# One block for layers 2 and 3 of a four-layer image kernel: offsets, sampling weights and padded images of layer 3 made during layer 2's attention

## The chip, the cores and the metric

The kernel runs on one core of one Trainium2 chip. Its time is the device time of one execution in microseconds (us); lower is better. Times are medians of repeated runs on the chip, and the profile is one execution taken by the hardware profiler. The engines are TensorE (PE, whose weight loads the trace lists as PEld), VectorE (DVE), ScalarE (ACT), GpSimd (POOL) and SyncE (SP, which issues DMA transfers here). Each engine runs its own instruction list in order and meets the others at semaphores.

## The reference

The input is 16 images of 64 channels and 16 x 16 places, in float32. Four layers follow each other, each as `x = x + layer(norm(x))`, where the norm is a group norm over pairs of channels of one image:

```python
x = x + _L0_conv_ref(_gn(x), ...)        # pointwise conv, mixture of basis functions
x = x + _L1_conv_ref(_gn(x), ..., 16, 16) # depthwise conv and linear state mixing
x = x + _L2_conv_ref(_gn(x), ...)        # attention, 8 heads of 8, over the 256 places of an image
x = x + _L3_conv_ref(_gn(x), ...)        # deformable 3 x 3 convolution
```

Layer 2 is `softmax(q k^T / sqrt(8)) v` for every image and head, and a projection. Layer 3 makes, by an ordinary 3 x 3 convolution of the normed image, two offsets and one mask (a sigmoid) for each of nine taps and each place. It then samples the normed image at the shifted, fractional places (bilinear), multiplies by the mask, and contracts the nine taps and 64 channels with a weight. Everything is per image: no image's result needs another image.

## The kernel before

Two images lie in one tile of 128 partitions (64 channels each), so there are 8 pairs of images. The layers run one after the other, each in a block with one instruction list per engine.

**Layer 2 (`layer2`, lines 761 to 1105).** The queries and keys are split into bfloat16 parts, stored to DRAM and loaded back as stacks (`k_st`, `q_st`). Then one pipeline runs over steps `v` from -19 to 143, eight steps per image, the same loop on every engine. At step `v` TensorE makes the scores that give the row maxima of step `v + 19` (line 1034) and the scores of step `v` (line 1047), and in four of eight steps the product of exponents and values (line 1067). VectorE takes the maxima (line 910), ScalarE the exponents (line 965). Each image's maxima go by POOL (lines 869, 871) and four small DMAs on SP (line 837) back into a row of `q_st`; SP then waits until they have landed, and step 8 of the image's scores may not start before. Maxima end at step 108, scores at step 127. Line 929 adds the attention of one image to `x`.

**Layer 3 (`layer3`).** It begins when layer 2's block has ended. A group norm of all images is followed by padded copies (`xpad`), which DMAs lay out as `stack`, four images a group. `conv_offsets(g)` (lines 1463, 1465) makes a group's offsets and masks. A chunk is four images too. For a chunk, hats are computed: `relu(1 - |position - row or column|)` for each tap and place (ACT lines 1376 and 1382), times the mask, then split into three bfloat16 parts (ACT, with POOL or DVE) and sent by DMA as `hats`. Positions reach `hat` by DMA through DRAM (`load_positions`, `load_masks`); only two thirds of the first chunk's are spread by matmuls instead (lines 1472, 1477).

The sampling loop runs over 8 pairs `n` and 9 taps `t`: TensorE spreads the hats (lines 1500, 1510), ACT copies one product (line 1404), DVE multiplies (line 1335), and TensorE contracts (line 1523). In six taps of each pair it also weighs the next pair's image (line 1491). A chunk serves two pairs; its hats are made by ACT and POOL while the chunk before is sampled.

## Time and profile before

| | us |
|---|---|
| median of 3 runs | 527.64 (525.78 to 527.82) |
| the profiled execution's span | 528.0 |
| attention pipeline, from its first exponent to the last addition | 233.7 to 347.2 |
| from there to the first multiplication of the sampling loop | 347.2 to 383.6 |
| sampling loop, to its last addition | 383.6 to 522.8 |
| the result to DRAM | 522.8 to 528.0 |

| engine | busy us | share of span |
|---|---|---|
| PE | 439.1 | 83% |
| DVE | 342.4 | 65% |
| ACT | 288.9 | 55% |
| POOL | 132.8 | 25% |

Shares over the whole span say little here, since the stages differ. The rows further down are read by stage. A timeline row gives the start, the duration, the engine and line, the operation, and in square brackets how long the engine sat idle before it and what ended that. A matmul of float32 appears as two records.

### The profile page before, as it was taken

The numbers are of one execution on the slowest core, as the hardware profiler recorded it, in microseconds if no ns is written. First come the engines' busy times: TensorE is split into PE (matmuls) and PEld (weight loads), VectorE is DVE, ScalarE is ACT, GpSimd is POOL, SyncE is SP. The second block draws the span as 40 slices with busy tenths as digits, with TensorE's granted clock in tenths as the row PEclk, the third lists the DMA queues.
The fourth block names the chain that finished last, engine by engine and source line by source line (L and its number), as shares of the span: only waits on it lengthen the run. The fifth ranks groups of instructions, "written<-read, shape, count | busy, mean of one in ns | idle before, by whom it ended". The sixth has DMA issues, their size and how long they took to land. (4 is left out here: it accounts for less than half of the span.)

```text
span 528.0 us, 9368 instructions
## 1 busy us (share of the span) xinstructions
PE 439.1 (83%) x3406; PEld 231.3 (44%) x3406; DVE 342.4 (65%) x668; ACT 288.9 (55%) x511; POOL 132.8 (25%) x162
## 2 busy tenths in 40 slices
PE   0527768899999887679999999939898999999995
PEld 0216648555455664223333333324443454454442
DVE  4549876233344568978999996251654778777784
ACT  1279955131532437047878778722865578486441
POOL 4420004000000005744422212031364428065000
PEclk9956997999999988559999999957977999999999
DMA  5500000900000004952200000016390480933302
GB/s 142 164 0 1 0 0 1 197 1 1 0 1 0 1 0 107 279 175 67 73 27 3 3 2 4 0 47 160 100 226 15 89 181 2 217 55 68 67 2 79
DMA packets 20767, 33.79 MB, mean 64 GB/s; under 512 B 5657, under 2 KB 15497, under 8 KB 19957
## 3 DMA queue, kind: packets, MB, share of 16 engines
q1 hardware_dynamic: 16724, 23.70, 18.9%
q0 software_dynamic: 2176, 6.35, 4.3%
q10 hardware_dynamic: 1824, 3.19, 2.3%
q8 instruction: 26, 0.43, 0.4%
q14 instruction: 17, 0.13, 0.1%
HBM read 16.21 MB, written 4.64 MB: 39 GB/s over the span
## 5 line engine op out<-in xcount | busy, mean ns | idle before, releaser
L1335 DVE TENSOR_TENSOR L_s<-L_row_ps,L_cols 128x1024 f32<-128x1024 f32 x72 | 87.6, 1218 | 9.3 <-PE L_row_ps L1500 7.5
L910 DVE TENSOR_REDUCE L_mx<-L_ring 128x2 f32<-128x512 f32 x128 | 83.3, 686 | 12.4 <-PE L_ring L1034 11.8
L965 ACT ACTIVATE L_e<-L_ring 128x512 f32<-128x512 f32 x128 | 73.7, 597 | 21.4 <-PE L_ring L1047 19.3
L1523 PE MATMUL L_acc<-L_s,L_t_sb 128*64 128x256 f32 x576 | 81.6, 406 | 1.1 <-DVE L_s L1335 1.0
L1404 ACT ACTIVATE L_cols<-L_col_ps 128x512 f32<-128x512 f32 x72 | 42.8, 596 | 48.9 <-PE L_col_ps L1510 48.5
L1034 PE MATMUL L_ring<-stacks_k_st,stacks_q_st 64*128 64x256 bf16 x256 | 51.0, 301 | 7.0 <-DMA stacks_k_st<-L_k_parts 4.7
L1523 PEld LDWEIGHTS L_acc<-L_s,L_t_sb 128*64 128x64 f32 x576 | 36.0, 140 | 35.9 <-DVE L_s L1335 19.8
L1047 PE MATMUL L_ring<-stacks_q_st,stacks_k_st 64*128 64x256 bf16 x256 | 47.2, 282 | 1.2 <-DMA stacks_q_st<-L_m_parts 1.2
L1500 PE MATMUL L_row_ps<-L_hats,L_sel 48*128 48x512 bf16 x144 | 44.6, 392 | 0.0
L1067 PE MATMUL L_ctx_ps<-L_e,L_v_x 128*32 128x256 f32 x512 | 41.5, 398 | 0.0
L1311 DVE COPY L_t_sb<-L_acc 128x192 f32<-128x192 f32 x48 | 17.1, 357 | 31.4 <-PE L_acc L1491 31.4
L1034 PEld LDWEIGHTS L_ring<-stacks_k_st,stacks_q_st 64*128 64x128 bf16 x256 | 15.9, 98 | 43.8 <-DVE L_mx L910 24.2
L382 PE MATMUL L_y<-L_t,all_w_post 128*128 128x256 f32 x96 | 25.3, 418 | 11.5 <-DVE L_t L342 11.5
L1510 PE MATMUL L_col_ps<-L_hats,L_sel 48*128 48x512 bf16 x72 | 28.7, 400 | 7.0 <-DMA L_hats<-L_parts 5.0
L1491 PE MATMUL L_acc<-all_w_all,L_xn 64*128 64x192 f32 x96 | 26.8, 362 | 5.0 <-DVE L_t_sb L1311 2.7
L382 PEld LDWEIGHTS L_y<-L_t,all_w_post 128*128 128x128 f32 x96 | 19.4, 208 | 17.1 <-DVE L_t L342 14.2
L1491 PE MATMUL L_col_ps<-all_w_all,L_xn 64*128 64x192 f32 x96 | 26.7, 360 | 0.0
L853 POOL MEMSET L_v_x<- 128x1024 f32 x1 | 1.0, 951 | 101.7 <-POOLq L496 101.7
L1200 POOL TENSOR_TENSOR L_hat<-L_hat,L_mask 64x768 f32<-64x768 f32 x9 | 16.3, 1812 | 40.1 <-ACT L_hat L1382 40.1
L415 ACT ACTIVATE L_uu<-L_z,L_minus_mu,L_inv 128x256 f32 x48 | 24.4, 586 | 1.3 <-DVEq L314 1.3
L633 ACT ACTIVATE L_sq<-L_t_ps 128x1024 f32<-128x1024 f32 x4 | 4.1, 1024 | 34.9 <-PE L_t_ps L716 34.9
L656 PE MATMUL L_xs_ps<-L_stack,L_w_tap 128*128 128x512 f32 x48 | 22.7, 601 | 0.0
(270 smaller groups left out, 814.2 us busy)
## 6 DMA issues: line engine op xcount, KB each, us to landing
L_hats<-L_parts SPq DMA_DIRECT2D x28, 216.0 KB, 5.0
L_hat<-L_offsets SPq DMA_DIRECT2D x20, 192.0 KB, 4.7
L_mask<-L_offsets SPq DMA_DIRECT2D x10, 192.0 KB, 4.9
stacks_q_st<-L_q_parts SPq DMA_DIRECT2D x12, 128.0 KB, 3.9
stacks_k_st<-L_k_parts ACTq DMA_DIRECT2D x12, 128.0 KB, 4.8
stacks_q_st<-L_q_parts POOLq DMA_DIRECT2D x12, 128.0 KB, 2.7
stacks_k_st<-L_k_parts POOLq DMA_DIRECT2D x12, 128.0 KB, 2.9
L_stack<-L_xpad SPq DMA_DIRECT2D x7, 162.0 KB, 5.8
```

The source lines that it names most:

```text
L382: mm = pe.matmul(y2[:, ds(k, 1), :], w_post[:], t[:, q, j:j + 1, :], start=False, stop=(j == NB - 1))
L910: dve.tensor_reduce(mx[:, n % 2, :, head], ring[:, place(step) % 3].rearrange("p (q s) -> p q s", q=2), AX.X, ALU.max).then_inc(max_read, 1)
L965: act.activation(e[:, k], ring[:, 3 + v % 3], ACT.Exp, scale=HD2 ** -0.5).then_inc(e_ready, 1)
L1034: mm = pe.matmul(ring[:, place(step) % 3, q * N:(q + 1) * N], rows_of(q_st, n, h, p)[:, q * P:(q + 1) * P], rows_of(k_st, n, h, p), start= ...
L1047: mm = pe.matmul(ring[:, 3 + v % 3, t * N:(t + 1) * N], rows_of(k_st, c, h, p)[:, t * P:(t + 1) * P], rows_of(q_st, c, h, p), start=True, ...
L1067: mm = pe.matmul(ctx_ps[32 * j:32 * j + 32, g * N:(g + 1) * N], v_x[:, c % 2, t, 4 * g + j, :], e[:, 4 * g + j, t * N:(t + 1) * N], start= ...
L1335: dve.tensor_tensor(s[:, q], row_ps[:, q], cols[:, t % 3:t % 3 + 1].broadcast_to([P, 2, 2 * N]), ALU.mult).then_inc(s_ready, 1)
L1404: act.activation(cols[:, v % 3], col_ps[:, c % 2], ACT.Copy).then_inc(col_read, 1)
L1491: mm = pe.matmul(out, xn[rows, b, k // 3 * P:(k // 3 + 1) * P], w_all[rows, k % 3 * TW:(k % 3 + 1) * TW], start=True, stop=True)
L1500: mm = pe.matmul(row_ps[:, v % 2, h], sel[0:3 * H, h], hats[0:3 * H, n % 2, :, t * N:(t + 1) * N], start=True, stop=True)
L1510: pe.matmul(col_ps[:, c % 2], sel[C:C + 3 * H, 2], hats[C:C + 3 * H, n % 2, :, t * N:(t + 1) * N], start=True, stop=True).then_inc(col_rea ...
L1523: mm = pe.matmul(acc[C * e:C * e + C, b, 0:N], t_sb[:, b, h, (KK * e + t) * C:(KK * e + t + 1) * C], s[:, q, h, e * N:(e + 1) * N], start= ...
```

## The change

`layer2` and `layer3` become one function, `layers2and3`, with one block. Layer 3's work is placed by step numbers into the attention loop:

- Line numbers: the parts that stay have new ones. Layer 3's tiles lie over layer 2's where these are done (`hats` over `k_st`, `xpad` and `sig` over `q_st`, `hat` and `parts` over layer 2's `parts`).
- **Norm.** The norm of layer 3 is made for four images at a time: DVE exchanges neighbouring channels' statistics (`stream_shuffle`) and aggregates, at steps 44, 76, 108 and 140. POOL takes the power -0.5, and writes `xpad` and the first two pairs' normed images. In the kernel before, DVE, TensorE and ACT did this for all images after layer 2.
- **Offsets.** Group 0's convolution stands on TensorE at step 58 in one piece; those of groups 1 and 2 in seven pieces at steps 112 to 118 and 120 to 126; group 3's in the sampling loop at pair 1, tap 0. The sigmoid is made as a tanh on ACT and a multiply-add on POOL.
- **First hats.** All positions come by DMA; the matmuls that spread them and their weight `to_places` are gone. ACT makes chunk 0's hats at steps 82 to 92, POOL multiplies the masks, DVE splits the parts at steps 109 to 120.
- **First weighing** at steps 114 to 124, the first spreads of the sampling loop at step 134.
- **SP** carries all transfers of layer 3, between the maxima and after them.

```diff
+    FIRST_OFFSETS = 58
+    OFFSETS = (None, 112, 120)
+    FIRST_HATS, FIRST_SPLIT, FIRST_WEIGHTS, FIRST_SPREAD = 82, 109, 114, 134
+    LAST_OFFSETS = (1, 0)
...
-                with sp.Fori(0, NQ) as i:
-                    for j in range(4):
-                        send_maxima(i, j)
+                for n in range(B):
+                    send_maxima(n)
+                    if n == 7:
+                        send_stack(0)
+                    if n == 8:
+                        store_offsets(0)
+                    if n == 9:
+                        load_places(0)
+                    if n == 11:
+                        send_stack(1)
+                send_stack(2)
+                store_offsets(1)
+                send_hats(0, 0)
+                send_hats(0, 1)
+                load_places(1)
+                store_offsets(2)
+                send_stack(3)
+                load_places(2)
+                send_hats(1, 0)
...
+                def norm_x(g):
+                    two = slice(2 * g, 2 * g + 2)
+                    pool.wait_ge(mv_ready, 2 * g + 2)
+                    step(pool.tensor_scalar(var[:, two], mv[:, two, 1], 1.0, EPS, ALU.mult, ALU.add))
+                    step(pool.tensor_tensor(scale[:, two], var[:, two], minus_half[:], ALU.pow))
...
                 for n in range(B):
...
+                    if n == 6:
+                        pool.wait_ge(s_ready, 32)
+                        pool.memset(xpad[:], 0.0).then_inc(edge_ready, 1)
+                        pool.wait_ge(edge_ready, 2)
+                        norm_x(0)
+                        pad_x(0)
+                    if n == 7:
+                        for p in range(2):
+                            pool.tensor_scalar(xn3[:, p, :], x[:, p, :], scale[:, p:p + 1], shift[:, p:p + 1], ALU.mult, ALU.add).then_inc(xn3_ready, 1)
+                    if n == 8:
+                        gate(0)
+                    if n == 10:
+                        norm_x(1)
+                        pad_x(1)
+                    if 11 <= n < 14:
+                        weigh_hat(pool, 0, n - 11)
+                    if n == 14:
+                        norm_x(2)
+                        pad_x(2)
...
+                    if v % 32 == 12 and v > 12:
+                        norm_stats(v // 32 - 1)
+                    if 0 <= v - FIRST_SPLIT < 12:
+                        split_hat(*divmod(v - FIRST_SPLIT, 4))
...
+                    if v == FIRST_OFFSETS + 1:
+                        act.wait_ge(off_conv, 1)
+                        take_offsets(0, ring[:, place["offsets", 0] % 3, 0:N])
+                    if 0 <= v - FIRST_HATS < 12 and (v - FIRST_HATS) % 2 == 0:
+                        j, part = divmod((v - FIRST_HATS) // 2, 2)
+                        (take_distance, make_hat)[part](0, j)
...
+                    if v == FIRST_OFFSETS:
+                        bank_free(("offsets", 0))
+                        for piece in range(7):
+                            conv_offsets(0, ring[:, place["offsets", 0] % 3, 0:N], piece)
```

TensorE's list around step 58, as it stood in the kernel before (steps 57, 58 and the start of 59; `stacks_...` are the attention's operands, L1067 the exponents times the values):

```order
L1034 MATMUL L_ring<-stacks_k_st,stacks_q_st 128x256 [waits L2_max_read]
L1034 MATMUL L_ring<-stacks_k_st,stacks_q_st 128x256
L1047 MATMUL L_ring<-stacks_q_st,stacks_k_st 128x256 [waits L2_e_ready]
L1047 MATMUL L_ring<-stacks_q_st,stacks_k_st 128x256
L1067 MATMUL L_ctx_ps<-L_e,L_v_x 32x256 x4
L1034 MATMUL L_ring<-stacks_k_st,stacks_q_st 128x256 [waits L2_max_read]
L1034 MATMUL L_ring<-stacks_k_st,stacks_q_st 128x256
```

And the same place now, where L1384, L1396 and L1414 are the former L1034, L1047 and L1067:

```order
L1384 MATMUL L_ring<-stacks_k_st,stacks_q_st 128x256 [waits L2_max_read]
L1384 MATMUL L_ring<-stacks_k_st,stacks_q_st 128x256
L1396 MATMUL L_ring<-stacks_q_st,stacks_k_st 128x256 [waits L2_e_ready]
L1396 MATMUL L_ring<-stacks_q_st,stacks_k_st 128x256
L1414 MATMUL L_ring<-L_e,L_v_x 32x256 x4
L1445 MATMUL L_ring<-L_stack,all_w_off 32x256 [waits L3_stack_in0,L2_max_read]
L1445 MATMUL L_ring<-L_stack,all_w_off 32x256 x23
L1447 MATMUL L_ring<-all_grid,all_w_grid 32x256 x4
L1384 MATMUL L_ring<-stacks_k_st,stacks_q_st 128x256 [waits L2_max_read]
```

The 28 matmuls of group 0's offsets stand between step 58 and step 59, and the first of them waits for the padded images to have landed (`L3_stack_in0`).

POOL's list of images 6 to 8 before (the maxima's two parts, the values):

```order
L869 CAST L_m_parts<-L_m_neg 8x256
L871 TENSOR_TENSOR L_m_parts<-L_m_neg,L_m_parts 8x256
L874 COPY L_v_x<-L_v_all 128x16x8
L869 CAST L_m_parts<-L_m_neg 8x256
L871 TENSOR_TENSOR L_m_parts<-L_m_neg,L_m_parts 8x256
L874 COPY L_v_x<-L_v_all 128x16x8
```

And now, from image 6's values to image 7's maxima:

```order
L1030 COPY L_v_x<-L_v_all 128x16x8
L1039 MEMSET L_xpad 128x1296
L992 ISA
L992 TENSOR_SCALAR L_var<-L_mv 128x2
L993 TENSOR_TENSOR L_scale<-L_var,L_minus_half 128x2
L994 TENSOR_SCALAR L_shift<-L_mv 128x2
L995 TENSOR_TENSOR L_shift<-L_shift,L_scale 128x2
L1003 TENSOR_SCALAR L_xpad<-all_x,L_scale,L_shift 128x16x16 x2
L1025 CAST L_m_parts<-L_m_neg 8x256
L1027 TENSOR_TENSOR L_m_parts<-L_m_neg,L_m_parts 8x256
```

Seven operations of layer 3 stand ahead of the two that make image 7's maxima.

SP's list in the second half of the attention, which before held nothing but the 64 small transfers of the maxima:

```order
L903 DMA stacks_q_st<-L_m_parts 1x4x256 x32
L914 DMA L_stack<-L_xpad 64x2x324
L915 DMA L_stack<-L_xpad 64x2x306
L914 DMA L_stack<-L_xpad 64x2x324
L915 DMA L_stack<-L_xpad 64x2x306
L903 DMA stacks_q_st<-L_m_parts 1x4x256 x4
L919 DMA L_offsets<-L_off 128x256
L921 DMA L_masks<-L_sig 128x256
L903 DMA stacks_q_st<-L_m_parts 1x4x256 x4
L928 DMA L_hat<-L_offsets 64x1x2304 x2
L928 DMA L_mask<-L_masks 64x1x2304
L903 DMA stacks_q_st<-L_m_parts 1x4x256 x8
```

Transfers of layer 3 now stand between those of images 7, 8, 9 and 10.

## Rows read from the trace of the kernel before

**Rows 1.** Busy time by stage: stretch, length, PE, PEld, DVE, ACT, POOL, granted clock, DMA share, GB/s.

```profile
250.00:326.00 76.00, 72.62 (x824) 29.91 (x825) 69.42 (x138) 61.50 (x122) 18.91 (x42) 1.00 0.08 22
326.00:347.20 21.20, 18.03 (x166) 7.53 (x164) 5.04 (x18) 13.33 (x27) 1.34 (x3) 0.96 0.01 1
347.20:383.60 36.40, 27.19 (x282) 14.96 (x283) 16.37 (x45) 18.30 (x31) 12.69 (x20) 0.78 0.45 113
```

**Rows 2.** Timeline of DVE, last addition of layer 2 and the sampling loop.

```profile
346.75 0.49 DVE L929 SCALAR_TENSOR_TENSOR all_x<-L_a_ps,all_l_vec,all_x 64x256 f32<-64x256 f32 x1 [1.90 <-PE L_a_ps L1089]
...
383.64 2.36 DVE L1335 TENSOR_TENSOR L_s<-L_row_ps,L_cols 128x1024 f32<-128x1024 f32 x2 [1.31 <-ACT L_cols L1404]
...
407.46 1.23 DVE L1335 TENSOR_TENSOR L_s<-L_row_ps,L_cols 128x1024 f32<-128x1024 f32 x1 [0.95 <-PE L_row_ps L1500]
...
423.51 2.55 DVE L1335 TENSOR_TENSOR L_s<-L_row_ps,L_cols 128x1024 f32<-128x1024 f32 x2
...
439.52 2.50 DVE L1335 TENSOR_TENSOR L_s<-L_row_ps,L_cols 128x1024 f32<-128x1024 f32 x2
...
522.36 0.48 DVE L1339 SCALAR_TENSOR_TENSOR all_x<-L_acc,all_l_vec,all_x 128x256 f32<-128x256 f32 x1 [1.19 <-PE L_acc L1523]
```

**Rows 3.** Timeline of TensorE: offsets of group 2, one weighing, next offsets.

```profile
373.71 2.77 PE L1463 MATMUL L_row_ps<-L_stack,all_w_off 128*32 128x256 f32 x48
...
376.85 0.43 PE L1491 MATMUL L_acc<-all_w_all,L_xn 64*128 64x192 f32 x1
...
377.38 2.80 PE L1463 MATMUL L_row_ps<-L_stack,all_w_off 128*32 128x256 f32 x48
```

**Rows 4.** Timeline of TensorE in the attention after the maxima have ended.

```profile
335.52 0.64 PE L1067 MATMUL L_ctx_ps<-L_e,L_v_x 128*32 128x256 f32 x8
336.09 0.39 PE L1047 MATMUL L_ring<-stacks_q_st,stacks_k_st 64*128 64x256 bf16 x2
```

**Rows 5.** Timeline of TensorE at step 58 and after.

```profile
281.48 0.64 PE L1067 MATMUL L_ctx_ps<-L_e,L_v_x 128*32 128x256 f32 x8
282.06 0.28 PE L1034 MATMUL L_ring<-stacks_k_st,stacks_q_st 64*128 64x256 bf16 x1
```

**Rows 6.** Timeline of ACT: one third of a hat.

```profile
375.75 0.92 ACT L1376 ACTIVATE L_hat<-L_hat,all_l_vec 128x768 f32<-128x768 f32 x1
376.70 0.84 ACT L1382 ACTIVATE L_hat<-L_hat 128x768 f32<-128x768 f32 x1
```

**Rows 7.** Timeline of POOL: maxima of image 7, a memset.

```profile
272.06 0.39 POOL L869 CAST L_m_parts<-L_m_neg 8x256 bf16<-8x256 f32 x1 [3.37 <-ACT L_m_neg L971]
272.53 0.66 POOL L871 TENSOR_TENSOR L_m_parts<-L_m_neg,L_m_parts 8x256 bf16<-8x256 f32 x1
...
347.99 2.26 POOL L428 MEMSET L_xpad<- 128x2592 f32 x1 [16.89 <-POOLq L823]
```

**Rows 8.** SP's issues for image 15; then first and last end of SP's waits for landing.

```profile
328.69 2.80 SPq L837 DMA_DIRECT2D stacks_q_st<-L_m_parts x4
...
L839 SPq EVENT_SEMAPHORE x16: 17/17/17, 233.0 to 332.6; - x16
```

**Rows 9.** DMA issues: transfer, queue, count, size of each, median us to landing.

```profile
L_stack<-L_xpad SPq DMA_DIRECT2D x7, 162.0 KB, 5.8
L_stack<-L_xpad ACTq DMA_DIRECT2D x1, 153.0 KB, 4.0
```

**Rows 10.** Busy time and granted clock after one wait of TensorE, and under transfers.

```profile
398.00:400.00 2.00, 0.19 (x1) 0.00 (x0) 0.17 (x1) 1.23 (x2) 0.24 (x1) 0.98 0.00 0
400.00:406.00 6.00, 5.84 (x26) 3.10 (x28) 2.46 (x4) 4.11 (x9) 3.20 (x2) 0.50 0.01 3
...
423.00:430.00 7.00, 7.00 (x54) 3.06 (x52) 5.63 (x7) 5.04 (x9) 0.58 (x1) 1.00 1.07 245
```

**Rows 11.** Timeline of DVE: one cast ahead of a POOL subtraction, one beside it.

```profile
203.29 0.43 DVE L895 CAST L_parts<-L_e 128x512 bf16<-128x512 f32 x1
...
206.25 1.26 DVE L895 CAST L_parts<-L_e 128x512 bf16<-128x512 f32 x1
```

More of the change, by code:

```diff
@@ L45, in ds @@
     return bass.ds(start, size)
-def from_turn(n, first):
-    return not isinstance(n, int) or n >= first
 class Memory:
@@ new lines, in send_hats @@
+                def send_hats(c, b):
+                    sp.wait_ge(parts3_ready, 3 * c + 3)
+                    if c:
+                        sp.wait_ge(product_used, KK * (2 * (c - 1) + b) + 10)
+                    else:
+                        sp.wait_ge(s_ready, 96)
+                    for k in range(2):
+                        for half in range(2):
+                            first = C * k + 2 * b + half
+                            sp.dma_start(hats[C * k:C * k + 3 * H, b, half], parts3[first:C * k + C:CH]).then_inc(hats_in[b], 16)
@@ L935, in _, with add_samples @@
+                def add_samples(n):
+                    dve.wait_ge(product_used, KK * n + KK + 2)
+                    dve.scalar_tensor_tensor(out=x[:, n, :], in0=acc[:, n % 2, 0:N], scalar=vec3[:, 2:3], in1=x[:, n, :],
+                                             op0=ALU.add, op1=ALU.add).then_inc(added, 1)
                 for v in ROWS:
@@ L1090, in project, with conv_offsets @@
                     mm.then_inc(o_ready, 1)
+                def conv_offsets(g, out, k, ready=off_conv):
+                    if k == 0:
+                        pe.wait_ge(stack_in[g], 64)
+                    for j in range(4):
+                        if k < 6:
+                            mm = pe.matmul(out[32 * j:32 * j + 32], w_off[:, k, :], tap(stack, CH * (g % 2) + j, k), start=(k == 0), stop=False)
+                        else:
+                            mm = pe.matmul(out[32 * j:32 * j + 32], w_grid[:], grid[:], start=False, stop=True)
+                    if k == 6:
+                        mm.then_inc(ready, 1)
@@ new lines, in weigh_first @@
+                def weigh_first(k):
+                    if k == 0:
+                        pe.wait_ge(xn3_ready, 1)
+                    else:
+                        pe.wait_ge(first_read, 2 * k)
+                    for half in range(2):
+                        rows = slice(C * half, C * half + C)
+                        pe.matmul(ring[:, 1 + half, 0:TW], xn3[rows, 0, k // 3 * P:(k // 3 + 1) * P], w_all[rows, k % 3 * TW:(k % 3 + 1) * TW],
+                                  start=True, stop=True).then_inc(first_ready, 1)
@@ new lines, in samples @@
+                def samples(n, b, t):
+                    u, q = KK * n + t, (b + t) % 2
+                    pe.wait_ge(product_ready, u + 3)
+                    if t == 0:
+                        pe.wait_ge(added, n + 1)
+                        if n:
+                            pe.wait_ge(col_read, col_at["weighed", 6 * n + 5] + 1)
+                        pe.wait_ge(first_read, 6 * n + 12)
+                    for h in range(2):
+                        for half in range(2):
+                            mm = pe.matmul(acc[C * half:C * half + C, b, 0:N], t_sb[b][:, h, (KK * half + t) * C:(KK * half + t + 1) * C],
+                                           products[:, q, h, half * N:(half + 1) * N], start=(t == 0 and h == 0), stop=(t == KK - 1 and h == 1))
+                    mm.then_inc(product_used, 1)
@@ L1564, in _, with program @@
                             if k == 0:
-                                pe.wait_ge(xn_ready, n + 2)
+                                pe.wait_ge(xn3_ready, n + 2)
                                 pe.wait_ge(added, n + 2)
-                            weigh(1 - n % 2, 6 * n + 6 + k, c + 1, k)
+                            weigh(1 - n % 2, 6 * (n + 1) + k, k)
+                        if (n, t) == LAST_OFFSETS:
+                            at = col_at["offsets", 3]
+                            pe.wait_ge(col_read, at - 1)
+                            for piece in range(7):
+                                conv_offsets(3, col_ps[:, at % 2, 0:N], piece, col_ready)
                         samples(n, n % 2, t)
-def col_step(t, more):
-    return t + sum(w < t for w in WEIGHED) if more else t
-def program(nc, ins, out, layers=4):
+def program(nc, ins, out):
     Memory.semaphores = ExitStack()
```

759 lines of the change are left out of this document (341 added, 418 removed).

## The prediction

> **What bounds the kernel now.** The stages come first, then the engine that ends each of them, then what would stand beside the moved work. By stage [rows 1], layer 2's attention keeps TensorE busy for 72.6 of 76.0 us and DVE for 69.4, at full clock: both are near their limit, and ACT, at 61.5, has a fifth of its time free. From the last addition of layer 2, which ends at 346.75 + 0.49 = 347.24, to the first multiplication of the sampling loop at 383.64 [rows 2] lie 36.4 us in which TensorE is busy for 27.2 at a mean clock of 0.78 of full [rows 1]: layer 3's preparation, a chain over all engines and DMAs. The loop then takes 522.84 - 383.64 = 139.2 us. Its first pair takes 407.46 - 383.64 = 23.8, its third 439.52 + 1.28 - 424.84 = 16.0, where 424.84 is the second multiplication of the row at 423.51 [rows 2]. So 7.8 us of the first pair are waits for hats. The second pair takes 424.84 - 407.46 = 17.4, which is 1.4 us of waiting where a new chunk begins; that stands three times in the loop, at its three new chunks. Without waits the loop would take 139.2 - 7.8 - 3 x 1.4 = 127.2.
>
> **What goes.** The preparation of 36.4 us and most of the 7.8. The norm's chain, the padding, the sigmoid's table and the matmuls that spread the positions are no longer waited for. What is left of them is paid for in the attention, where an engine is already full.
>
> **What the attention gains in length.** I follow each added piece on the engine that is full there.
>
> *Offsets on TensorE.* A group's convolution takes from 373.71 to 376.85 [rows 3], 3.1 us at full clock, and three groups now stand in the attention. That TensorE has room once the maxima have ended is not so: a step with exponents times values takes 281.48 to 282.06 = 0.58 us for that product with the maxima's matmuls there [rows 5], and 335.52 to 336.09 = 0.57 without them [rows 4]; the scores take their time either way. So all of it lengthens the attention: 3.1 at step 58, and 2 x 3.1 = 6.2 at steps 112 to 126. The first weighing is six pairs of matmuls at 377.38 - 376.85 = 0.53 [rows 3]: 3.2 us. DVE's copies out of it are not on the path as long as its splits keep pace (below).
>
> *The wait at step 58.* The first of the 28 matmuls waits for the stack. Step 59 starts at 282.06 [rows 5], a step lasts 76 us / 11 images / 8 = 0.86, so step 44 starts at about 269.1. DVE follows a step behind, adds a maximum and four small operations: statistics at 271.7 at the earliest. POOL then has four tiny operations (none has a row; 0.2 us each, half of what 256 elements take) and two of 256 elements a lane, for which the two forms of 256 elements give 0.39 and 0.66 [rows 7]; I take 0.5. That is 273.5, and image 7's maxima, which started at 272.06, come after it: 1.1 us more, 274.6. The memset of half the size, 1.1 us [rows 7], lies before the statistics. SP's four issues for maxima and their landing take 332.6 - 328.69 = 3.9 [rows 8]: 278.7. Four issues of the stack at 0.7 (2.80 / 4) follow, the last out at 280.8; it lands 4.0 us later where one queue sends little, 5.8 as the median [rows 9]. TensorE is there at 282.7. The wait is 2.1 to 3.9 us, zero if POOL is quicker than thought; I take 2.3, near the first row, since little else is being sent.
>
> *The clock after it.* TensorE stood for almost 2 us at 398 to 400, and the next 6 us have a granted clock of 0.50, its lower level of 1.2 GHz [rows 10]. A wait of 2.3 us would bring the same: a half-clock stretch of 6 to 7 us costs half of itself, 3.4.
>
> *Statistics.* Four more operations on DVE in the path at steps 44 and 76; a shuffle has no row, and with 0.15 to 0.4 us each a group costs about 0.6: 1.2 together. The third group's lie at the end of the maxima and cost nothing.
>
> *Hats on ACT.* A third takes 376.70 - 375.75 = 0.95 and 0.84 [rows 6], three thirds 5.4 us, in 12 steps of 10.4 us. ACT's free fifth of these is 2.0; one step, 0.9, is absorbed by the banks between ACT and TensorE: 2.5 us. Between zero (all absorbed) and 5.4.
>
> *Maxima behind large transfers.* SP sends positions and masks of chunk 0, 3 x 0.59 MB, between image 9's and image 10's maxima. At 245 GB/s [rows 10] they take 7.2 us, about 8.7 with issue and landing. Image 10's maxima, due 6.9 after image 9's, would land up to 2.3 us late, and TensorE can bear 2.0: image 15's landed at 332.6 [rows 8], and its first step stands one step before that of 335.52 [rows 4]. I take 1.0; the bounds are 0 and 7.2. The Trainium skill (DMA: Bandwidth & Descriptors, Queues, rings and completion order) says that each DMA engine consumes a queue's descriptors in ring order. By that rule the maxima cannot pass the positions; if they could, this term would be 0. No row before shows the two behind each other.
>
> Sum: 3.1 + 6.2 + 3.2 + 2.3 + 3.4 + 1.2 + 2.5 + 1.0 = 22.9. The attention ends at 347.24 + 22.9 = 370.1.
>
> **The loop.** Its first multiplication is now made before the attention's last addition, its second about 0.6 us after; that is as if the first stood a mean step of 16.0 / 9 = 1.8 before, at 368.9. Are chunk 0's hats there? DVE's twelve split operations are six casts, 0.43 x 768 / 512 = 0.65 each [rows 11], and six subtractions of 768, 0.9 each (three quarters of 1.18, the multiplication of 1024 [rows 2]): 9.3 us, in twelve steps that TensorE's added work stretches from 10.4 to about 16. They end near step 121, the sending takes about 8 us, and step 134 comes 10 us after: in time by 2 us. Chunk 1's positions are issued right behind and land about when the loop starts. Group 3's offsets add 3.1 us in pair 1 and by that cover the first of the three chunk waits; two of 1.4 stay, since the order of hats on ACT and POOL is the same. Last, the attention ends with little for TensorE to do: the mean clock of 0.96 over 21.2 us [rows 1] means 1.7 us at the lower level before 347.2. The loop therefore starts at half clock, for 3.0 us. So the loop takes 127.2 + 3.1 + 2.8 + 3.0 = 136.1 and ends at 505.0; with 528.0 - 522.84 = 5.2 for the result, 510.2. The profiled span of 528.0 lies 0.4 above the median of the runs, so I forecast 510.
>
> **Rivals.**
>
> *Clean overlap.* The stack lands in time (its issue leaves two steps of margin if POOL's operations take 0.3), no clock falls, ACT absorbs two more us: 510.2 - 2.3 - 3.4 - 1.5 - 1.0 - 3.0 = 499. For it: POOL idles 3.37 us ahead of image 7's maxima [rows 7]. Against it: the attention leaves no engine a margin of more than two us.
>
> *A cascade on SP.* One queue serves everything in order, with a blocking wait per image. If the maxima of two more images come 3 us late, each with a half-clock stretch, that is 2 x (3.0 + 3.4): 523. Against it: after image 10 SP has only one stack to send before image 15.
>
> *Splits slowed.* A cast took 1.26 instead of 0.43 us where a POOL subtraction ran beside it [rows 11]. With all six slowed, 1.9 instead of 0.65 each, the splits end 7.5 us later; 2 to 3 of these are margin, the hats hold back step 134 by 5: 515. The Trainium skill (SBUF — State Buffer, Who interferes with whom) has a rule for it: casts in a two-port mode and POOL exclude each other for whole instructions, and the loser waits. The two rows agree. By that rule only the casts that meet POOL's padding of group 2 and image 15's maxima are hit, some 3 us of POOL's work, and the sum stays as it is.
>
> *Slower.* POOL's power operation has no row. It stands ahead of the maxima of images 7, 11 and 15, where the margin is 2.0 us. If the norm of a group takes over 2.0 us longer than I think, each excess is paid three times; 8 us an operation gives 510 + 3 x 8 = 534. It decides from 6 us on, (528 - 510) / 3. Against it: only two elements a lane.
>
> **How the numbers follow.** The forecast (504 to 516 with its own bounds: no clock loss at one of the two places, -3.4, and a little less on ACT; or the stack's wait at 3.9 and two us more on SP) has 0.45. Clean overlap 0.20, the cascade 0.18, slowed splits 0.10, the slow power operation 0.07. The range takes in all but the last and the outer edges: 497 to 524. A change under 0.5% cannot be told from none: faster means under 525. All cases but the last lie there, less 0.03 for a longer cascade: 0.90 faster. The last is 0.06 slower, and 0.04 remain for within 0.5%.
>
> **What would show it.** Right: TensorE's offsets of group 0 wait for the stack, then the lower clock; the attention's last addition near 370; the loop near 136 us. Wrong: a last addition before 362 (the added work was hidden), hats that hold back step 134, or POOL rows of several us for the power. The forecast falls if one of the added waits in the attention is longer than 6 us.

## The result, and the profile after

The changed kernel takes 510.19 us (median of 4 runs, 508.70 to 512.79) against 526.71 for the kernel before on the same chip (4 runs, 525.52 to 527.82): a ratio of 0.9676, 95% interval 0.9644 to 0.9707. It was forecast at 510 and faster.

The profiled execution took 509.65 us; its span is 507.9, and every execution's time is about 1.8 us above its span. The stages of the changed kernel, in the columns of [rows 1]:

```profile
250.00:326.00 76.00, 70.27 (x792) 29.16 (x788) 62.12 (x132) 57.90 (x116) 29.03 (x57) 0.98 0.24 61
326.00:368.80 42.80, 37.44 (x385) 16.00 (x383) 25.96 (x63) 22.61 (x45) 9.76 (x15) 0.96 0.50 111
369.90:502.70 132.80, 128.63 (x1007) 64.06 (x1003) 100.81 (x121) 81.26 (x156) 48.51 (x34) 1.00 0.34 75
```

The preparation of 36.4 us between attention and loop [rows 1, 2] is gone. In the first row TensorE is busy for 70.27 of 76 us, less than the 72.62 before, though it was given a convolution: new pauses have come in.

The sampling loop's first and second multiplication and the last addition, now:

```profile
367.01 1.23 DVE L1167 TENSOR_TENSOR L_products<-L_ring,L_cols 128x1024 f32<-128x1024 f32 x1 [0.35 <-issue]
...
369.90 2.38 DVE L1167 TENSOR_TENSOR L_products<-L_ring,L_cols 128x1024 f32<-128x1024 f32 x2
...
502.19 0.48 DVE L1171 SCALAR_TENSOR_TENSOR all_x<-L_ring,all_l_vec,all_x 128x256 f32<-128x256 f32 x1 [1.19 <-PE L_ring L1497]
```

How much longer the attention has become, and where, is read from DVE's addition of each finished image. First the kernel before, images 3, 4, 5, 7, 8, 9 and 11 (image 15 stands in [rows 2]); start, duration, line:

```profile
269.38 0.49 DVE L929 SCALAR_TENSOR_TENSOR all_x<-L_a_ps,all_l_vec,all_x 64x256 f32<-64x256 f32 x1
276.40 0.47 DVE L929 SCALAR_TENSOR_TENSOR all_x<-L_a_ps,all_l_vec,all_x 64x256 f32<-64x256 f32 x1
283.21 0.49 DVE L929 SCALAR_TENSOR_TENSOR all_x<-L_a_ps,all_l_vec,all_x 64x256 f32<-64x256 f32 x1
...
297.03 0.49 DVE L929 SCALAR_TENSOR_TENSOR all_x<-L_a_ps,all_l_vec,all_x 64x256 f32<-64x256 f32 x1
304.05 0.47 DVE L929 SCALAR_TENSOR_TENSOR all_x<-L_a_ps,all_l_vec,all_x 64x256 f32<-64x256 f32 x1
310.86 0.49 DVE L929 SCALAR_TENSOR_TENSOR all_x<-L_a_ps,all_l_vec,all_x 64x256 f32<-64x256 f32 x1
...
324.69 0.49 DVE L929 SCALAR_TENSOR_TENSOR all_x<-L_a_ps,all_l_vec,all_x 64x256 f32<-64x256 f32 x1
```

The same images in the changed kernel, and image 15:

```profile
268.26 0.49 DVE L1123 SCALAR_TENSOR_TENSOR all_x<-L_ring,all_l_vec,all_x 64x256 f32<-64x256 f32 x1
275.68 0.47 DVE L1123 SCALAR_TENSOR_TENSOR all_x<-L_ring,all_l_vec,all_x 64x256 f32<-64x256 f32 x1
289.14 0.49 DVE L1123 SCALAR_TENSOR_TENSOR all_x<-L_ring,all_l_vec,all_x 64x256 f32<-64x256 f32 x1
...
302.96 0.49 DVE L1123 SCALAR_TENSOR_TENSOR all_x<-L_ring,all_l_vec,all_x 64x256 f32<-64x256 f32 x1
311.20 0.47 DVE L1123 SCALAR_TENSOR_TENSOR all_x<-L_ring,all_l_vec,all_x 64x256 f32<-64x256 f32 x1
318.60 0.49 DVE L1123 SCALAR_TENSOR_TENSOR all_x<-L_ring,all_l_vec,all_x 64x256 f32<-64x256 f32 x1
...
332.42 0.49 DVE L1123 SCALAR_TENSOR_TENSOR all_x<-L_ring,all_l_vec,all_x 64x256 f32<-64x256 f32 x1
...
368.32 0.49 DVE L1123 SCALAR_TENSOR_TENSOR all_x<-L_ring,all_l_vec,all_x 64x256 f32<-64x256 f32 x1
```

From one end (start plus duration) to the next:

| from image to image | before | after | longer by | what was added there |
|---|---|---|---|---|
| 3 to 4 | 7.00 | 7.40 | 0.40 | statistics of group 0 |
| 4 to 5 | 6.83 | 13.48 | 6.65 | convolution 0, the wait for its stack, the clock |
| 5 to 7 | 13.82 | 13.82 | 0.00 | nothing |
| 7 to 8 | 7.00 | 8.22 | 1.22 | statistics of group 1, maxima behind the positions |
| 8 to 9 | 6.83 | 7.42 | 0.59 | first hats on ACT |
| 9 to 11 | 13.83 | 13.82 | -0.01 | hats' end |
| 11 to 15 | 22.06 | 35.90 | 13.84 | convolutions 1 and 2, first weighing, splits |
| sum | | | 22.7 | forecast 22.9 |

In the step from image 7 to 8 TensorE waits for image 10's maxima, which stand behind the positions on SP:

```profile
307.80 0.39 PE L1396 MATMUL L_ring<-stacks_q_st,stacks_k_st 64*128 64x256 bf16 x2 [0.53 <-DMA stacks_q_st<-L_m_parts]
```

TensorE's two waits for a stack, at steps 58 and 120 of the changed kernel (in brackets the idle time ahead and what ended it), and then the granted clock right after each:

```profile
283.16 4.46 PE L1445 MATMUL L_ring<-L_stack,all_w_off 128*32 128x256 f32 x48 [1.75 <-DMA L_stack<-L_xpad]
...
350.40 0.64 PE L1445 MATMUL L_ring<-L_stack,all_w_off 128*32 128x256 f32 x8 [2.29 <-DMA L_stack<-L_xpad]
```

```profile
283.00:287.00 4.00, 3.84 (x41) 2.13 (x44) 0.00 (x0) 0.00 (x0) 0.00 (x0) 0.57 0.02 5
...
350.00:355.00 5.00, 4.60 (x40) 1.76 (x44) 0.62 (x2) 1.33 (x3) 0.00 (x0) 0.66 0.86 194
```

4 x (1 - 0.57) = 1.7 and 5 x (1 - 0.66) = 1.7 us are lost to the lower of the two levels, 1.2 GHz. The wait at step 58 had been forecast; the one at 120 had not. What stands ahead of its stack is POOL's norm and padding of group 2, then image 15's maxima:

```profile
335.73 0.87 POOL L994 TENSOR_SCALAR L_shift<-L_mv 128x2 f32<-128x2 f32 x1
...
337.30 2.88 POOL L1003 TENSOR_SCALAR L_xpad<-all_x,L_scale,L_shift 128x256 f32<-128x256 f32 x2
340.13 0.39 POOL L1025 CAST L_m_parts<-L_m_neg 8x256 bf16<-8x256 f32 x1
```

For group 0, with no split on DVE, the same two lines took 0.19 and 1.10 us. In the loop, at each new chunk, DVE waits before the first copy of the next pair's weighed products (the "first thought" of an expectation below; 0.39 where nothing is late):

```profile
403.23 0.36 DVE L1160 COPY L_t_sb<-L_ring 128x192 f32<-128x192 f32 x1 [1.91 <-PE L_ring L1467]
...
436.49 0.36 DVE L1160 COPY L_t_sb<-L_ring 128x192 f32<-128x192 f32 x1 [1.64 <-PE L_ring L1467]
...
469.73 0.36 DVE L1160 COPY L_t_sb<-L_ring 128x192 f32<-128x192 f32 x1 [1.62 <-PE L_ring L1467]
```

So 1.5, 1.25 and 1.2 us above normal: all three chunk waits are there.

### The profile page after: what moved, and what is told of

Read it like the earlier page. It is cut to its first block, busy times and chain, and to the rows that moved or that the text cites. A ratio compares the mean times of both kernels' runs of the same rounds, so it can differ in the third digit from the quotient of the medians.

```text
span 507.9 us, 9178 instructions
## 1 busy us (share of the span) xinstructions
PE 424.9 (84%) x3378; PEld 223.2 (44%) x3378; DVE 340.9 (67%) x674; ACT 277.7 (55%) x496; POOL 138.7 (27%) x172
## 3 DMA queue, kind: packets, MB, share of 16 engines
q1 hardware_dynamic: 17296, 26.84, 22.1%
## 4 chain that ended last, share of the span: by engine, by line
PE 31%; DMA 8%; POOL 7%; DVE 5%; SPq 3%; ACT 3%; issue 3%; ACTq 1%; POOLq 0%; DVEq 0%
PE L_ring L1497 9%; PE L_ring L1414 5%; PE L_ring L1474 4%; PE L_ring L1384 4%; DMA L_hats<-L_parts 3%; DMA stacks_q_st<-L_m_parts 2%; POOL L_parts L1018 2%; PE L_ring L1445 2%; PE L_ring L1467 2%; POOL L_rest L1014 2%; SPq L903 1%; ACTq L881 1%; DMA L_stack<-L_xpad 1%; DVE L_mx L1104 1%; PE L_ring L1396 1%
## 5 line engine op out<-in xcount | busy, mean ns | idle before, releaser
L1167 DVE TENSOR_TENSOR L_products<-L_ring,L_cols 128x1024 f32<-128x1024 f32 x72 | 87.7, 1219 | 8.8 <-PE L_ring L1474 7.9
L1497 PE MATMUL L_ring<-L_products,L_t_sb 128*64 128x256 f32 x576 | 78.0, 392 | 0.6 <-DVE L_products L1167 0.5
L1277 ACT ACTIVATE L_cols<-L_ring 128x512 f32<-128x512 f32 x72 | 42.8, 596 | 48.7 <-PE L_ring L1484 48.3
L1384 PE MATMUL L_ring<-stacks_k_st,stacks_q_st 64*128 64x256 bf16 x256 | 51.3, 302 | 6.5 <-DVE L_v_all L1090 4.3
L1396 PE MATMUL L_ring<-stacks_q_st,stacks_k_st 64*128 64x256 bf16 x256 | 48.7, 285 | 1.9 <-DMA stacks_q_st<-L_m_parts 1.9
L1497 PEld LDWEIGHTS L_ring<-L_products,L_t_sb 128*64 128x64 f32 x576 | 34.9, 136 | 33.7 <-DVE L_products L1167 19.8
L1474 PE MATMUL L_ring<-L_hats,L_sel 48*128 48x512 bf16 x144 | 43.4, 381 | 0.6 <-DVE all_x L1123 0.6
L1414 PE MATMUL L_ring<-L_e,L_v_x 128*32 128x256 f32 x512 | 42.2, 404 | 0.5 <-ACT L_e L1227 0.5
L1384 PEld LDWEIGHTS L_ring<-stacks_k_st,stacks_q_st 64*128 64x128 bf16 x256 | 16.0, 99 | 43.9 <-DVE L_mx L1104 24.2
L889 POOL TENSOR_TENSOR L_hat<-L_hat,L_mask 64x768 f32<-64x768 f32 x12 | 21.9, 1825 | 41.9 <-ACT L_hat L1260 41.9
L1484 PE MATMUL L_ring<-L_hats,L_sel 48*128 48x512 bf16 x72 | 27.7, 386 | 3.0 <-DMA L_hats<-L_parts 3.0
L1160 DVE COPY L_t_sb<-L_ring 128x192 f32<-128x192 f32 x42 | 15.0, 358 | 22.3 <-PE L_ring L1467 22.3
L1467 PE MATMUL L_ring<-all_w_all,L_xn 64*128 64x192 f32 x168 | 29.0, 324 | 0.0
L1467 PEld LDWEIGHTS L_ring<-all_w_all,L_xn 64*128 64x128 f32 x168 | 23.5, 189 | 1.7
L655 PE MATMUL L_xs_ps<-L_stack,L_w_tap 128*128 128x512 f32 x48 | 22.7, 601 | 0.0
```

The costliest lines, as they stand in the source:

```text
L1167: dve.tensor_tensor(products[:, q], row_ps[q], cols[:, t % 3:t % 3 + 1].broadcast_to([P, 2, 2 * N]), ALU.mult).then_inc(product_ready, 1)
L1277: act.activation(cols[:, v % 3], col_ps[:, at % 2], ACT.Copy).then_inc(col_read, 1)
L1384: mm = pe.matmul(ring[:, place["largest", step] % 3, q * N:(q + 1) * N], rows_of(q_st, n, h, p)[:, q * P:(q + 1) * P], rows_of(k_st, n, h, ...
L1396: mm = pe.matmul(ring[:, 3 + v % 3, t * N:(t + 1) * N], rows_of(k_st, c, h, p)[:, t * P:(t + 1) * P], rows_of(q_st, c, h, p), start=True, ...
L1414: mm = pe.matmul(ctx_ps[32 * j:32 * j + 32, g * N:(g + 1) * N], v_x[:, c % 2, t, 4 * g + j, :], e[:, 4 * g + j, t * N:(t + 1) * N], start= ...
L1467: pe.matmul(out, xn3[rows, b, k // 3 * P:(k // 3 + 1) * P], w_all[rows, k % 3 * TW:(k % 3 + 1) * TW], start=True, stop=True).then_inc(read ...
```

## Experiments

Ratios are to the kernel before, with 95% intervals. Terms are compared inside profiles, from image to image, since whole executions of one kernel spread over some 5 us (what goes with that is shown below). All runs but the last four named ran on one chip, whose mark is the repeated kernel at 511.92 us.

**The changed kernel again.** Expected: 

> The changed kernel once more, unedited, as the mark for the other runs of this chip: 510 us, 0.968 of the kernel before.

Measured: 511.92 us (508.77 to 514.15), 0.9707 (0.9670 to 0.9744). This execution lost what the first had not: a stretch at half clock at the loop's start. First this one, then the first one, the same 7 us of program:

```profile
368.00:375.00 7.00, 6.41 (x28) 2.19 (x28) 4.26 (x11) 2.75 (x4) 2.66 (x7) 0.52 0.14 42
```

```profile
367.50:374.50 7.00, 6.12 (x46) 3.08 (x47) 5.89 (x13) 4.46 (x8) 4.16 (x7) 1.00 0.22 61
```

Same instructions, and the same pauses of TensorE ahead (0.66, 0.20, 0.59 and 0.59 us in both): 28 matmuls in one, 46 in the other. The loop from the first product, which is the first multiplication (367.15 and 367.01), to the last addition's end takes 138.3 against 135.7.

**Group 0's convolution two steps later.**

```diff
-    FIRST_OFFSETS = 58
+    FIRST_OFFSETS = 60
```

Expected: 

> One number: the convolution of group 0 stands at step 60 in place of 58, some 2.3 us later. Theory (the stack lands 1.75 us too late for step 58, and this pause takes the clock to 0.5 for 3.4 us, which costs another 1.7): both go, attention's last addition comes 3.4 us earlier, 506.7 us. Rival 1 (the pause is covered: what follows it, exponentials and contexts, catches up): 510, no change. Rival 2 (the offsets and so the first hats come later, and the hats wait for their places at step 82): 510 to 512.

Measured: 508.29 us (506.76 to 512.27), 0.9666 (0.9631 to 0.9700): 3.6 us below the repeated kernel.

```profile
283.40 2.80 PE L1445 MATMUL L_ring<-L_stack,all_w_off 128*32 128x256 f32 x48 [0.50 <-DMA L_stack<-L_xpad]
```

The wait is 0.50 and the 48 matmuls take 2.80 us, not 4.46. Images 4 to 6 take 17.4 us instead of 20.5: 3.1 of the 3.4. Rivals 1 and 2 fall; the wait lay on the path with its clock.

**Splits after POOL's padding.**

```diff
-    FIRST_HATS, FIRST_SPLIT, FIRST_WEIGHTS, FIRST_SPREAD = 82, 109, 114, 134
+    FIRST_HATS, FIRST_SPLIT, FIRST_WEIGHTS, FIRST_SPREAD = 82, 113, 114, 134
```

Expected: 

> One number: VectorE's twelve parts of the splitting of the first hats start at step 113 in place of 109, which is after GpSimd's padding of group 2. Theory (VectorE's casts slow GpSimd's padding, 2.88 us instead of 1.10; so the maxima of image 15, behind it on GpSimd, are late, and behind them on SyncE the stack of group 2, for which TensorE waits 2.3 us at step 120, with 3.4 us at clock 0.5 after it): the paddings fall back to 1.1 us, the stack is issued about 4 us earlier, and 2.3 + 1.7 = 4.0 us go: 506 us. Rival 1 (GpSimd is slow there for another reason, such as the convolutions or SyncE's transfers): paddings stay at 2.9 us, 510. Rival 2 (the stack comes early but the first hats, 4.7 us later, become the wait at step 134): the wait at 120 goes and one of 1 to 4 us appears before the first product: 508 to 511.

Measured: 516.97 us (514.33 to 518.24), 0.9801 (0.9774 to 0.9827): slower than the changed kernel. POOL's padding, and then ACT at the loop's start:

```profile
336.88 1.10 POOL L1003 TENSOR_SCALAR L_xpad<-all_x,L_scale,L_shift 128x256 f32<-128x256 f32 x2
```

```profile
376.29 0.93 ACT L1256 ACTIVATE L_hat<-L_hat,all_l_vec 128x768 f32<-128x768 f32 x1 [7.18 <-DMA L_mask<-L_masks]
```

The cause is shown: without splits beside it the padding takes 1.10 instead of 2.88, the stack leaves at 342.64 instead of 344.84, and the wait at 120 is 0.56. The first two operations of the splits still run ahead of it, and show that not only casts hold POOL up. An operation that took 0.19 us for group 0 here took 0.86, to 336.49, beside a subtraction of DVE that ended at 336.44:

```profile
335.63 0.86 POOL L994 TENSOR_SCALAR L_shift<-L_mv 128x2 f32<-128x2 f32 x1
```

```profile
335.48 0.96 DVE L1148 TENSOR_TENSOR L_rest<-L_hat,L_parts 128x768 f32<-128x768 f32 x1
```

Rival 2 had the place of the new wait (the first product now waits 1.27 us), but none of the theories had the price. The later hats leave SP's queue later, and behind them the positions of chunk 1 (363.42 instead of 355.78). ACT waits 7.2 us for these, and the loop's columns stand behind it on ACT.

**Padding behind image 15's maxima on POOL.**

```diff
-                    if n == 14:
+                    if n == 15:
                         norm_x(2)
                         pad_x(2)
```

Expected: 

> GpSimd takes the statistics and the padding of group 2 behind the maxima of image 15 and not ahead of them; VectorE's splitting stays at step 109. Theory (what holds up the stack of group 2 is SyncE's order: it stands behind the maxima of image 15 and waits for them to land): the maxima of image 15 go out about 5 us earlier, the padding stays slow (2.9 us) but the stack goes out about 3 us earlier, and the wait of 2.3 us at step 120 goes, with at least part of the half clock behind it: 506 to 508 us. Rival (it is the slow padding alone that is late, whatever stands ahead of it): the stack goes out within 1 us of where it did, 509 to 510.

Measured: 512.37 us (509.06 to 513.32), 0.9721 (0.9697 to 0.9745); the wait at 120 is 2.27. The maxima's cast starts at 334.41 instead of 340.13, but the stack leaves at 344.04 instead of 344.84: POOL's copy of the values, which waits for the context before, now stands ahead of the padding (it ran at 338.86). The rival's sign came out (the stack within 1 us of where it was, no gain beside the repeated kernel's 511.92), for another reason than it gave.

**Both convolutions later.**

```diff
-    FIRST_OFFSETS = 58
-    OFFSETS = (None, 112, 120)
+    FIRST_OFFSETS = 60
+    OFFSETS = (None, 112, 123)
```

Expected: 

> The convolution of group 0 at step 60 in place of 58, and that of group 2 at steps 123 to 129 in place of 120 to 126; nothing else. Theory (both stacks then have landed, so the pauses of 1.75 and 2.3 us go, and with each the half clock that cost 1.7): attention's last addition 7.4 us earlier than in the changed kernel, 503 to 504 us beside 510 to 512. Rival 1 (the pause at step 120 is covered by the exponentials' and VectorE's lag, so that only step 60 counts): 507 to 508. Rival 2 (group 2's offsets, 4 us later, hold up the first spreading or the places of chunk 2): 507 or more, with a wait for ScalarE's offsets before the first product.

Measured: 506.91 us (503.36 to 507.71), 0.9578 (0.9539 to 0.9617). Images 4 to 15 take 86.1 instead of 92.7 us: 6.6 of the 7.4. The median falls by 5.0 us from the repeated kernel's. In the profile a part of the gain is lost again: the loop from the first product takes 139.6 us instead of 135.7, because it now begins before chunk 1's positions have landed:

```profile
367.42 0.93 ACT L1256 ACTIVATE L_hat<-L_hat,all_l_vec 128x768 f32<-128x768 f32 x1 [3.18 <-DMA L_mask<-L_masks]
```

**Idle matmuls in TensorE's pauses.** (`turn_back` transposes a context on TensorE.)

```diff
                         turn_back(c - 2)
+                        if c - 2 == B - 1:
+                            keep_clock(pe, avg2, ctx_ps, 2)
...
+                keep_clock(pe, avg2, ctx_ps, 2)
                 pe.wait_ge(o_added, B)
```

Expected: 

> Two idle matmuls (128x128, their result is never read) behind the last turning back of a context and two behind the last projection, in TensorE's pauses of 0.59 us each. Theory (the pauses at attention's end take the clock to 0.5 in some executions, as in the profiled one of the repeated kernel, 368 to 375, and not in others, as in the first; that is the spread of 509 to 514): clock 1.0 from 356 on in every execution, all times between 508.5 and 510, the median some 2 us down. Rival 1 (the clock falls for the sparser work before it, not for these pauses): the same spread, median 511 to 512. Rival 2 (the idle matmuls stand in the way of the projection and the first spreading): 0.2 to 0.5 us slower.

Measured: 507.23 us (506.07 to 509.39), 0.9621 (0.9586 to 0.9656). No half clock at the loop's start in the profile; whether that is the idle matmuls' doing is taken up again at the last run. The median fell by 4.7 us where 2 were expected, and the rest is not explained. The spread fell from 5.4 to 3.3 us, not to 1.5: this execution shows where the rest is. TensorE at step 58, and the clock behind it:

```profile
280.99 2.80 PE L1445 MATMUL L_ring<-L_stack,all_w_off 128*32 128x256 f32 x48 [1.76 <-DMA L_stack<-L_xpad]
```

```profile
281.00:285.00 4.00, 4.00 (x64) 2.55 (x64) 0.42 (x1) 0.38 (x1) 0.00 (x0) 1.00 0.02 5
```

The wait is 1.76 as before (1.75), yet the clock stays at 1.0, and images 4 to 5 take 11.81 instead of 13.48 us: the half clock costs 1.67, measured in two executions whose programs are the same up to there.

**Group 3's convolution behind the hats' last steps.**

```diff
-    LAST_OFFSETS = (1, 0)
+    LAST_OFFSETS = (1, 4)
```

Expected: 

> The convolution of group 3 behind tap 4 of pair 1 in place of tap 0, so behind the last three steps of chunk 1's hats on ScalarE. Theory (at tap 0 it delays these steps by its 3.1 us too, so that it covers nothing of the wait for chunk 1; behind them it covers it): the wait of 1.9 us before pair 2's first thought falls to 0.4 us, 1.5 us go: 508.5 to 510. Rival 1 (the hats of chunk 1 hang on GpSimd, not on ScalarE's steps): the wait stays at 1.9, no change. Rival 2 (the offsets of group 3 are then late for chunk 3): no change here, and a longer wait before pair 6.

Measured: 509.21 us (507.42 to 511.33), 0.9649 (0.9612 to 0.9687). DVE's waits around the convolution:

```profile
397.76 0.36 DVE L1160 COPY L_t_sb<-L_ring 128x192 f32<-128x192 f32 x1 [4.01 <-PE L_ring L1467]
...
401.51 0.36 DVE L1160 COPY L_t_sb<-L_ring 128x192 f32<-128x192 f32 x1 [0.39 <-PE L_ring L1467]
```

The wait of 1.91 at the new chunk is gone, the convolution's own is 4.01 - 0.39 = 3.6 instead of 3.1, and the loop from the first product is 1.1 us shorter in the profile (134.6, with 135.7 above). The theory holds, with 1.1 of its 1.5 us; in whole times that cannot be told from the spread.

**Fewer matmuls.**

```diff
-                        if 0 <= v - OFFSETS[g] < 7:
+                        if v - OFFSETS[g] in (0, 6):
```

Expected: 

> Leaves out five of the seven pieces of the convolutions of groups 1 and 2 (their offsets are then not the reference's): steps 113 to 117 and 121 to 125 lose 4 matmuls of 0.09 us each and more. Theory (attention there is bound by TensorE, every matmul put in lengthens it): 10 pieces of 0.44 us go, attention's last addition 4.4 us earlier: 506 to 507.5. Rival 1 (VectorE, with the splitting of the first hats, sets the pace from step 112 on): 0 to 1 us. Rival 2 (the wait for the stack at step 120 grows by what goes before it): about 2.2 us of the 4.4, 508 to 509.

Measured: 514.01 us (512.06 to 517.65), 0.9739 (0.9697 to 0.9782): leaving work out made it no faster than the repeated kernel (511.92). Around step 120, first this kernel and then, as the mark, the one before it in this list:

```profile
347.00:350.00 3.00, 0.20 (x4) 0.23 (x8) 0.05 (x1) 0.00 (x0) 0.32 (x1) 0.53 0.85 236
350.00:365.00 15.00, 13.84 (x83) 5.59 (x75) 3.30 (x11) 4.98 (x10) 0.00 (x0) 0.53 1.02 209
```

```profile
347.00:350.00 3.00, 0.70 (x11) 0.33 (x9) 1.38 (x3) 1.17 (x3) 0.83 (x1) 1.00 0.73 207
350.00:365.00 15.00, 14.10 (x146) 6.22 (x139) 3.77 (x12) 6.49 (x13) 0.41 (x1) 0.89 1.00 205
```

The stack lands when it lands (the wait grows from 2.30 to 3.71 us), the clock falls within this longer pause, and with less to do after it the clock stays at its lower level until 364. Rival 2 had the kind of loss (1.4 us of its 2.2), and none of the three had the longer half clock. It does not answer whether TensorE binds these steps, so the opposite was tried.

**The same pieces twice**, where no stack is waited for long.

```diff
                             conv_offsets(g, ring[:, 0, 0:N], v - OFFSETS[g])
+                            if 0 < v - OFFSETS[g] < 6:
+                                conv_offsets(g, ring[:, 0, 0:N], v - OFFSETS[g])
```

Expected: 

> The kernel with the convolutions at steps 60 and 123 (no long wait for a stack), in which five of the seven pieces of groups 1 and 2 are computed twice (their offsets are then not the reference's): ten pieces more, of four matmuls, 0.44 us each (a convolution alone takes 3.1 for seven). Theory (with the waits for stacks gone, attention's last images are bound by TensorE and each matmul lengthens them by its own time): attention's last addition 4.4 us later than at 123, in the steps of images 13 to 15. Rival (what leaving pieces out showed, that the clock and the wait for the stack set these steps, holds here too: the added pieces fill pauses): below 2 us.

Measured: 507.22 us (504.82 to 508.90), 0.9612 (0.9569 to 0.9655). Images 11 to 15 take 35.6 instead of 32.1 us: 3.5 of 4.4. So TensorE binds these steps, and a fifth of the added work falls into its pauses. In the whole time it shows hardly at all, since the wait for the positions of chunk 1 falls from 3.18 to 0.92 us.

**ACT's first hats over 32 of 768 columns.** The slice of `hat` in `take_distance` and `make_hat` is cut to 32 columns for chunk 0. Expected: 

> The changed kernel, in which ScalarE makes the first hats over 32 columns of each third's 768 (chunk 0's hats are then not the reference's): six instructions of 0.85 to 0.95 us at steps 82 to 92 shrink to about 0.2 each, 4 us of ScalarE go. Theory 1, as in the prediction (2.5 us of them lie on the path): images 9 and 10 end 2.5 us earlier. Theory 2, from the trace of the changed kernel, where image 9 ends only 0.6 us later than its shift before and image 10 none: 0.6 us.

Measured, in one profiled execution (512.84 us): ACT's first distance, and DVE's additions for images 8 and 9:

```profile
310.14 0.31 ACT L1257 ACTIVATE L_hat<-L_hat,all_l_vec 128x32 f32<-128x32 f32 x1
```

```profile
310.55 0.47 DVE L1124 SCALAR_TENSOR_TENSOR all_x<-L_ring,all_l_vec,all_x 64x256 f32<-64x256 f32 x1
317.36 0.49 DVE L1124 SCALAR_TENSOR_TENSOR all_x<-L_ring,all_l_vec,all_x 64x256 f32<-64x256 f32 x1
```

Image 9 comes 6.83 us after image 8, as in the kernel before, against 7.42: the hats cost 0.59, theory 2.

**Together.** To the edits at 60, 123, tap 4 and the idle matmuls comes one of SP's order:

```diff
                 send_hats(0, 0)
-                send_hats(0, 1)
                 load_places(1)
+                send_hats(0, 1)
```

Expected: 

> Together: group 0 at step 60, group 2 at step 123, group 3 behind tap 4 of pair 1, the idle matmuls at attention's end, and on SyncE's queue the places of chunk 1 between the two halves of the first hats (the half for odd pairs is needed only at pair 1). Theory (with 60 and 123 alone the loop's start then waits 3.2 us for these places, with a half clock behind it; four sends of 0.74 us ahead of them are what makes them late): that wait falls below 0.5 us, the wait for chunk 1's hats goes, and the time is 500 to 502.5 us. Rival (the places are late for the amount of data, 1.7 MB behind the hats, not for their place in the queue): the wait stays at 2 us or more and the time at 503 to 505.

Measured: 501.67 us (500.82 to 502.44), 0.9523 (0.9495 to 0.9550): faster than both kernels. The positions leave SP at 349.55, 4.2 us earlier than with 60 and 123 alone, and ACT starts on them without a wait:

```profile
363.37 0.94 ACT L1256 ACTIVATE L_hat<-L_hat,all_l_vec 128x768 f32<-128x768 f32 x1
```

The rival falls, since the positions' own 1.7 MB are the same: it was their place in the queue. Whether the four sends ahead of them held them up by the time of their issue or by their data was not separated.

**The same without the idle matmuls.** Expected: 

> The last version (501.67, six runs from 500.8 to 502.4) without its four idle matmuls at attention's end. Theory 1 (they keep the clock at 1.0 at the loop's start, where without them it falls to 0.5 for 3.4 us in some executions): the times spread again, from 501 to 504.5, the median 1 to 2 us up. Theory 2 (once the pauses at steps 58 and 120 are gone there is nothing for them to do): 501.0 to 502.5 as before, no half clock.

Measured: 503.80 us (502.91 to 505.60), 0.9563 (0.9540 to 0.9587). TensorE's pauses without them, then its clock; and the clock of the same 7 us with them:

```profile
359.88 0.65 PE L1436 MATMUL L_ring<-L_ctx_c,all_w_o 128*64 128x128 f32 x4 [0.60 <-ACT L_ctx_c L1239]
361.11 0.60 PE L1474 MATMUL L_ring<-L_hats,L_sel 48*128 48x512 bf16 x1 [0.59 <-DVE all_x L1123]
```

```profile
361.00:368.00 7.00, 6.89 (x29) 2.75 (x29) 3.45 (x10) 2.80 (x5) 3.88 (x7) 0.51 0.75 162
```

```profile
362.00:369.00 7.00, 6.84 (x54) 3.35 (x52) 5.59 (x14) 5.54 (x10) 4.17 (x7) 1.00 0.75 165
```

29 matmuls against 54 in 7 us: the half clock lasts about 7 us here, not 3.4. Theory 1 holds for the median (2.1 us; by the ratios to the kernel before 2.1 us too, which matters as this run and the last version ran on different chips); the spread grew from 1.6 to 2.7 only. One profile each would prove little, since the half clock also stays away without idle matmuls. Of the eleven profiles without them, seven have it at this place (a clock of 0.51 to 0.58 over 7 us) and four have not; of the two with them, none has it. The times of the two versions do not overlap.

## Why the prediction was right, point by point

The mechanism was right: the preparation went, and nearly all of the added work lengthened an attention that TensorE bounds. The total was closer than its terms, and a part of that is luck.

- **Which time was summed.** The sum of 510.2 was one of spans. The profiled span after is 507.9, so the sum was 2.3 us too long. The step that took the span for the time of a run (528.0 "0.4 above the median") hid 1.8 of it, as an execution's time lies 1.8 above its span; that is luck. Of the 2.3, the attention was 1.1 us ahead of the kernel before at image 3 already, where both still do the same; from run to run image 0 ends between 245.9 and 249.3.
- **Convolution 0, its wait and the clock:** forecast 3.1 + 2.3 + 3.4, measured 6.65 in all, of which the wait 1.75 and the clock 1.7. The half clock was sized by the 6 us of [rows 10]; here it lasted about half as long, and in two of the eight profiles with this step it did not come at all.
- **Statistics** 1.2 forecast, from prices of 0.15 to 0.4 us that no row had; the shuffles took 0.16 each, and image 4 came 0.40 later. **Maxima behind the positions** 1.0 forecast. In the 1.22 of image 8 both lie together. In the profile with group 0 at step 60 alone TensorE does not wait for the maxima there, and image 8 comes 0.43 later; so about 0.4 are the statistics and 0.8 the maxima. This second part is not steady: over the thirteen profiles it is 0 to 1.2 us.
- **Hats on ACT,** 2.5 forecast, 0.59 measured, and nearly all of it gone with narrow hats. The banks between ACT and TensorE absorb more than the one step that was granted them.
- **Convolutions 1 and 2 and the weighing,** 6.2 + 3.2 = 9.4 forecast. Measured 13.84, of which 2.29 + 1.7 are the wait at step 120 and its clock: 9.85. With both convolutions later, and so without that wait, the same images were 32.1 - 22.1 = 10.0 longer. The wait is the term that the sum lacked. That the sum came out is luck here: the 13.84 - 9.4 = 4.4 too little were made up by what was too large, 2.15 at convolution 0 (8.8 against 6.65), 1.9 for the hats and 0.6 for statistics and maxima.
- **The rival of slowed splits** had the right collision and the wrong loser: DVE's casts kept 0.55 us, POOL's padding went from 1.10 to 2.88. The Trainium skill (SBUF — State Buffer, Who interferes with whom) says of DVE's two-port modes that whichever of DVE and POOL starts first holds the shared pair of ports for a whole instruction and the other is blocked. The trace agrees for the casts: a POOL operation of 0.19 us that started at 336.68, during a cast (336.58 to 337.14), took 0.51 and ended 0.05 us after it. The padding's 1.10 without splits beside it shows the cause. The prediction had taken from this rule only what DVE would lose, and had counted casts alone; the subtractions hold POOL up too (0.86 instead of 0.19, above).
- **The loop:** forecast 136.1, measured 502.67 - 368.1 = 134.6, counted as in the prediction from 1.8 ahead of the second multiplication (369.90). The convolution's 3.1 came (127.2 + 3.1 + 4.0 = 134.3). The claim that it covers the first chunk wait failed: at tap 0 it delayed the hats' last three steps too, so all three waits stayed, 4.0 instead of 2.8. The 3.0 of half clock at the start did not come in this execution; they came in the next (138.3 - 135.7 = 2.6). The forecast put this term in whole, and it comes in some executions only.
- **The other rivals:** the power took 0.69 to 0.73 us, far under the 6 that would have decided; there was no cascade, and no clean overlap. Chunk 0's hats were there in time: no wait for them stands before the first product.

What stays open: why a half-clock stretch comes in one execution and not in the other behind the same pause. Whether the maxima's wait comes from the order in SP's queue or from the load on the DMA engines was not tried.

## What to carry to other kernels

When work is moved into a stage that one engine bounds, sum it on that engine, but follow also each queue that the moved work passes: the one term missing here was a chain POOL, SP, DMA behind a step that looked far from the bound. A wait for a transfer is removed most cheaply by placing its consumer two or three steps later (3.1 us for one number), and after each such gain the next thing in the same queue is late (positions at 3.2 us, and 7.2 where the hats went out later). Compare terms between milestones of profiles rather than whole times when single executions spread by more than the term.
